# Delta steps: 32-row products of the block inverse joined in pairs, dense sets divided by filter and value products

## The chip, the cores and the metric

The kernel runs on one core of a Trainium2 chip. Its time is device time in microseconds (us), the median of several executions. PE is TensorE (its matmuls), PEld its weight loads, DVE VectorE, ACT ScalarE, POOL GpSimd, and SP the queue that issues the DMAs.

## The reference

Two layers over 16 sequences of 512 tokens of 128 values, each layer an attention part and a feed-forward part. The change lies in the attention of the second layer, a gated delta rule with 16 heads of 64 values:

```python
qkv = silu(causal_conv4(x @ W_qkv));  beta = sigmoid(b);  g = -A * softplus(a + dt_bias)
q = l2norm(q) / 8;  k = l2norm(k)
def step(S, t):                              # per sequence and head, S is 64x64
    S = S * exp(g[t])
    S = S + outer(k[t], (v[t] - k[t] @ S) * beta[t])
    return S, q[t] @ S
y = rmsnorm(y) * norm_w * silu(z);  x = x + y @ W_o
```

## The kernel before

The program has five phases: front (first layer), gates, delta, attention with experts, and capacity. The delta phase walks 64 steps. A step takes one chunk of 64 tokens of two sequences at once (rows 0 to 63 and 64 to 127, `SEQS`), for all 16 heads. Within a chunk the rule becomes the solution of a triangular system of 64 rows per sequence and head, and the kernel builds the inverse of that system from blocks:

- POOL inverts the diagonal blocks of 16 rows (`L1383`, `L1387`), and SP carries blocks between `at`, `ablk`, `tblk`, `ti` and `tt` through DRAM.
- Two blocks of 16 make one of 32. There are two such joins per sequence, `BLOCKS = [(b, u)]`. First `at` times `ti` gives `w4` (L1612, 16 heads by four blocks); DVE masks it with a column of row flags `hi` (L1801). Then `tt` times `w4` (L1634, for `ti`) and `w4` times `tt` (L1638, for `tt`) are made head by head. DVE subtracts the one into `ti` (L1824, `t4_ready`), ACT copies the other negated into `tt` (L1452, `tt4_ready`).
- Two blocks of 32 make the whole: `w5` (L1649, copied by ACT at L1469) and L1659, copied by ACT at L1478. The system is then solved at L1682.

Every fp32 product is two weight loads and two matmuls in PE's stream, so that L1612 has 128 matmuls a step.

In the same step the other engines prepare later steps. The filter of q and k takes four blocks a step (`conv(p, u, e)`, e from 0 to 3, L1542): PE makes the product, ACT takes the last tap out of PSUM (L1406, `take_conv`), DVE adds the other three (L1761, `filter_block`, raising `conv_done`), ACT applies silu (L1418). Blocks 0, 2 and 3 use the same two PSUM banks, block 1 another two, so that `conv` waits at L1540, before block 3 until the filter of block 2 is done:

```python
hold(sem("conv_done"), done - 1 if e == 2 else done)
```

The value products `project_v` (L1567) are two halves of four taps each; `sum_squares` (L1580) is a product of 128 rows and 128 columns that moves two columns.

The order on each engine is written out by hand in `iteration`, and each engine goes through it in order; `hold` and `wait_ge` wait on semaphores. PE's order in a step is: state products (L1561), key products `kkq` (L1552), L1612, filter block 0, values half 0, filter block 1, L1634 with L1638, filter block 2, values half 1, L1649, filter block 3, L1659, z (L1665), `sum_squares(0)`, solve (L1682), transposes, update (L1708), L1561, output (L1717), `sum_squares(1)`, L1734. ACT's order around the filter is: block 0 taken, values half 0, silu of block 0, block 1 taken, the four copies of L1452, block 2 taken, silu of block 1, squares, values half 1, the copy of `w5`, block 3 taken. DVE's order is: L1776 and L1778 twice (which read the key products), L1796, L1801, L1806, L1813, filter of blocks 0 and 1, L1824, filter of block 2, L1832, L1834, L1838, filter of block 3. Steps 1 to 56 run in a loop of eight steps each; the last five steps have no filter products.

Of the kernel before, what the change touches and what calls it, by code (L numbers as in the profile page):

```python
# [6 lines left out]
ALU = mybir.AluOpType  # L7
# [3 lines left out]
P = 128  # L11
# [677 lines left out]
CH = 64  # L689
# [348 lines left out]
def delta_phase(nc, x_in, x_out, h_t, gates, decays, a_blocks, t_blocks, w_in, conv_t, norm_w, w_o):  # L1038
# [17 lines left out]
    with ExitStack() as ctx:  # L1056
# [5 lines left out]
        hi = sb("hi", [P, 1])  # L1062
# [34 lines left out]
        ti = sb("ti", [P, DH, HB + SB])  # L1097
        tt = sb("tt", [P, DH, CH])
        w4 = sb("w4", [P, DH, HB])
# [122 lines left out]
        def _(sp):  # L1222
# [42 lines left out]
            def iteration(p, u):  # L1265
# [33 lines left out]
                if have(p, u + 1):  # L1299
                    hold(sem("inverse"), i + 2)  # L1300
                    sp.dma_start(t_blocks[0].rearrange("n h r c -> (n h) r c"), tblk[:, 0, :, :]).then_inc(sem("ti_stored"), 16)
                    hold(sem("turned_back"), i + 2)
                    sp.dma_start(t_blocks[1].rearrange("n h r c -> (n h) r c"), tblk[:, 1, :, :]).then_inc(sem("tt_stored"), 16)
                    hold(sem("ti_stored"), 16 * (i + 2))
                    hold(sem("w5_sum"), i + 1)
                    for n in range(NBLK):
                        rows = slice(SB * n, SB * n + SB)
                        m = n % (CH // SB)
                        if m != 3:
                            c1 = SB if m == 1 else HB  # L1310
# [19 lines left out]
        def _(pool):  # L1330
# [23 lines left out]
            link(pool.tensor_tensor(hi[:, :], hk[:, 0:1], hk[:, 1:2], ALU.add))  # L1354
# [44 lines left out]
        def _(act):  # L1399
# [31 lines left out]
            def iteration(p, u):  # L1431
# [16 lines left out]
                if now:  # L1448
                    act.wait_ge(sem("t4_sum"), i + 1)
                    for b, w in BLOCKS:  # L1450
                        low = slice(64 * b + HB * w, 64 * b + HB * w + SB)
                        last = act.activation(tt[low, :, HB * w + SB:HB * w + HB],  # L1452
                                              pb[low, 1, DH * SB:2 * DH * SB].rearrange("p (h c) -> p h c", c=SB),
# [56 lines left out]
        def _(pe):  # L1510
# [54 lines left out]
            def project_v(p, u, m):  # L1565
                for t in range(TAPS):
                    last = pe.matmul(pa[:, B + m, :], hs[:, u % 2, t, :], wv[:, t, cols(m)],  # L1567
                                     start=(t == 0), stop=(t == TAPS - 1))
                last.then_inc(sem("v_sum"), 1)
# [14 lines left out]
            def iteration(p, u):  # L1584
# [9 lines left out]
                if then:  # L1594
# [9 lines left out]
                    kkq(p, u + 1, 1)  # L1604
                if now:
# [3 lines left out]
                    for h in range(DH):  # L1609
                        for b, w in BLOCKS:  # L1610
                            rows = rows_of(b, w)
                            last = pe.matmul(pb[rows, 0, h * SB:(h + 1) * SB], at[rows, u % 2, h, HB * w:HB * w + HB],  # L1612
                                             ti[rows, h, HB:HB + SB], start=True, stop=True)
                    last.then_inc(sem("w4_sum"), 1)
                if cv:
                    conv(p, u, 0)
                if then:
# [4 lines left out]
                    project_v(p, u + 1, 0)  # L1622
                if cv:
                    conv(p, u, 1)
                if now:
# [5 lines left out]
                    for h in range(DH):  # L1631
                        for b in SEQS:
                            rows = rows_of(b, 0)
                            last = pe.matmul(pb[rows, 0, (DH + h) * SB:(DH + h + 1) * SB], tt[rows, h, 0:HB], w4[rows, h, 0:SB],  # L1634
                                             start=True, stop=True)
                        for b, w in BLOCKS:
                            rows = rows_of(b, w)
                            last = pe.matmul(pb[rows, 1, (DH + h) * SB:(DH + h + 1) * SB], w4[rows, h, :],  # L1638
                                             tt[rows, h, HB * w + SB:HB * w + HB], start=True, stop=True)
                    last.then_inc(sem("t4_sum"), 1)  # L1640
# [78 lines left out]
                if far:  # L1719
                    hold(sem("n4_ready"), n + 1)  # L1720
                    hold(sem("q_squared"), n + 1)
                    sum_squares(1).then_inc(sem("q_summed"), 1)
                if now:
# [7 lines left out]
                    for m in HALVES:  # L1731
# [5 lines left out]
                        last.then_inc(sem("o_sum"), 1)  # L1737

# [3 lines left out]
        def _(dve):  # L1742
# [40 lines left out]
            def iteration(p, u):  # L1783
# [98 lines left out]
                if far:  # L1882
                    dve.wait_ge(sem("q_summed"), n + 1)
                    dve.tensor_scalar(tq[:, (u + 2) % 4, :], pb[:, 1, DH:2 * DH], DHD * RMS_EPS,
                                      DHD * RMS_EPS * L2_EPS, ALU.mult, ALU.add).then_inc(sem("tq_ready"), 1)
                if now:
# [8 lines left out]
                    last.then_inc(sem("o_ready"), 1)  # L1895
                made[part] += links[0]
# [739 lines left out]
```

## Time and profile before

| | us |
|---|---|
| median of 3 executions | 4637.02 |
| lowest, highest | 4636.9, 4659.84 |
| the profiled execution | 4655.05 |
| its span | 4653.3 |
| delta stage within the span, about | 1410 to 3960 |
| mean granted TensorE clock over the span | 0.897 |

The profile describes the one profiled execution, whose time is 18.03 us above the median. Its parts give the busy time of each engine, groups of instructions by line, waits by what ended them, and timelines. "issue" names idle time for which the profile shows no semaphore. PEclk is the granted TensorE clock: 1.00 is the higher level, 2.4 GHz, and 0.50 the lower, 1.2 GHz; other values are means over a stretch.

### The profile page before, as it was taken

The numbers are of one execution on the slowest core, as the hardware profiler recorded it, in microseconds if no ns is written. First come the engines' busy times: TensorE is split into PE (matmuls) and PEld (weight loads), VectorE is DVE, ScalarE is ACT, GpSimd is POOL, SyncE is SP. The second block draws the span as 40 slices with busy tenths as digits, with TensorE's granted clock in tenths as the row PEclk, the third lists the DMA queues.
The fourth block names the chain that finished last, engine by engine and source line by source line (L and its number), as shares of the span: only waits on it lengthen the run. The fifth ranks groups of instructions, "written<-read, shape, count | busy, mean of one in ns | idle before, by whom it ended". The sixth has DMA issues, their size and how long they took to land. (4 is left out here: it accounts for less than half of the span.)

```text
span 4653.3 us, 163745 instructions
## 1 busy us (share of the span) xinstructions
PE 3861.4 (83%) x66245; PEld 2812.4 (60%) x66245; DVE 3117.4 (67%) x6104; ACT 1733.8 (37%) x3495; POOL 1595.7 (34%) x2519
## 2 busy tenths in 40 slices
PE   6999999866648998989988989989899998588860
PEld 4666666533326776767776767767677766455530
DVE  3777777747746676767666766767677654288858
ACT  1222222224423343444443433434444432277750
POOL 1333333311004454444444444544444443100001
PEclk6998999988858999999999999999999987699975
DMA  0222222136522222222222222222222221111105
GB/s 25 44 47 46 55 56 49 42 84 155 158 65 49 42 56 41 47 51 48 50 47 49 48 49 40 57 42 47 51 48 49 49 47 26 55 27 28 28 18 149
DMA packets 695281, 251.77 MB, mean 54 GB/s; under 512 B 529368, under 2 KB 660128, under 8 KB 694176
## 3 DMA queue, kind: packets, MB, share of 16 engines
q1 hardware_dynamic: 694560, 241.62, 23.7%
q8 instruction: 518, 8.49, 0.8%
q14 instruction: 203, 1.66, 0.1%
HBM read 154.63 MB, written 86.79 MB: 52 GB/s over the span
## 5 line engine op out<-in xcount | busy, mean ns | idle before, releaser
L1373 POOL TENSOR_TENSOR d_f<-d_ms,d_mhalf 128x16 f32<-128x16 f32 x64 | 239.5, 3742 | 965.1 <-DVE d_ms L1807 965.1
L1567 PE MATMUL d_pa<-d_wv,d_hs 128*128 128x512 f32 x1024 | 517.6, 652 | 0.9 <-DVE d_qk L1778 0.4
L1761 DVE SCALAR_TENSOR_TENSOR d_acc<-d_pa,d_cq,d_acc 128x512 f32<-128x512 f32 x576 | 431.7, 750 | 95.2 <-ACT d_acc L1406 80.3
L1383 POOL TENSOR_TENSOR d_prod<-d_ablk,d_tblk 128x15 f32<-128x15 f32 (+7 forms) x960 | 342.5, 357 | 218.5 <-DMA d_ablk<-a_blocks 147.9
L1387 POOL TENSOR_TENSOR d_tblk<-d_tblk,d_prod 128x28 f32<-128x28 f32 (+7 forms) x896 | 336.4, 375 | 70.8 <-POOL d_prod L1383 0.2
L1567 PEld LDWEIGHTS d_pa<-d_wv,d_hs 128*128 128x128 f32 x1024 | 219.5, 215 | 232.1 <-issue 220.2
L1542 PE MATMUL d_pa<-d_hq,d_wqk 128*128 128x259 f32 x768 | 255.4, 462 | 81.4 <-DVE d_acc L1761 58.0
L1406 ACT ACTIVATE d_acc<-d_pa,d_cq 128x512 f32<-128x512 f32 x192 | 131.9, 687 | 420.8 <-PE d_pa L1542 418.0
L262 POOL TENSOR_TENSOR a_act<-a_act,a_cws 128x512 f32<-128x512 f32 x128 | 166.8, 1316 | 310.2 <-DMA a_cws<-cw_rows 165.3
L1580 PEld LDWEIGHTS d_pb<-d_of_head,d_sqT 128*128 128x128 f32 x2048 | 246.2, 196 | 39.2 <-issue 39.0
L1370 POOL TENSOR_TENSOR d_nr<-d_n,d_half_power 128x16 f32<-128x16 f32 x64 | 188.0, 2938 | 193.8 <-DVE d_n L1846 179.8
L1580 PE MATMUL d_pb<-d_of_head,d_sqT 128*128 128x2 f32 x2048 | 243.8, 250 | 0.6 <-ACT d_sqT L1411 0.5
L294 ACT ACTIVATE a_sil<-a_gp 128x512 f32<-128x512 f32 x144 | 86.1, 598 | 406.1 <-PE a_gp L367 403.6
L1761 DVE SCALAR_TENSOR_TENSOR d_acc<-d_pc,d_cq,d_acc 128x512 f32<-128x512 f32 x192 | 144.2, 751 | 130.5 <-ACT d_acc L1406 125.9
L1505 ACT ACTIVATE d_sq<-d_o 128x1024 f32<-128x1024 f32 x64 | 67.7, 1057 | 435.4 <-DVE d_o L1892 390.1
L1542 PEld LDWEIGHTS d_pa<-d_hq,d_wqk 128*128 128x128 f32 x768 | 149.8, 216 | 132.3 <-issue 111.3
L906 PE MATMUL g_pe<-g_gu,g_after 128*128 128x512 f32 x256 | 152.0, 725 | 89.7 <-DVE g_gu L966 89.7
L2208 PE MATMUL e_xp<-e_w,e_yT 128*128 128x512 f32 x256 | 151.6, 676 | 47.8 <-ACT e_part L2094 47.8
L1423 ACT ACTIVATE d_v<-d_pa 128x512 f32<-128x512 f32 x128 | 76.4, 597 | 301.9 <-PE d_pa L1567 288.2
L1418 ACT ACTIVATE d_kq<-d_acc 128x512 f32<-128x512 f32 x256 | 159.5, 623 | 73.1 <-DVE d_acc L1761 72.5
L369 PE MATMUL a_up<-a_bhT,a_wu 128*128 128x512 f32 x288 | 168.7, 671 | 13.3 <-DVE a_act L546 11.8
L1776 DVE TENSOR_TENSOR d_at<-d_dd,d_pa 128x512 f32<-128x512 f32 x128 | 87.6, 684 | 136.6 <-PE d_pa L1552 136.4
(371 smaller groups left out, 9418.3 us busy)
## 6 DMA issues: line engine op xcount, KB each, us to landing
a_cws<-cw_rows SPq DMA_DIRECT2D x32, 1024.0 KB, 10.5
decays<-g_dec SPq DMA_DIRECT2D x16, 2048.0 KB, 7.3
d_dd<-decays SPq DMA_DIRECT2D x64, 512.0 KB, 4.3
d_hs<-h_t SPq DMA_DIRECT2D x512, 32.0 KB, 2.2
t_blocks<-d_tblk SPq DMA_DIRECT2D x128, 128.0 KB, 1.7
a_blocks<-d_at SPq DMA_DIRECT2D x512, 16.0 KB, 1.9
d_ablk<-a_blocks SPq DMA_DIRECT2D x64, 128.0 KB, 2.1
d_tt<-t_blocks SPq DMA_DIRECT2D x512, 16.0 KB
```

Of the source, the lines that this page charges most:

```text
L262: pool.tensor_tensor(act_sb[:, b, :], act_sb[:, b, :], cws[:, m % 2, b, :], ALU.mult)\
L369: pe.matmul(up[:, :], wu[:, b, :], bhT[:, m % 2, :], start=True, stop=True).then_inc(sem("up_sum"), 1)
L906: last = pe.matmul(pe_[:, c % 2, m, :], after[:, :, :].rearrange("p b s -> p (b s)"), gu[:, c % 2, m * DH // 2:(m + 1) * DH // 2, :].rearr ...
L1370: pool.tensor_tensor(nr[:, :], n4[:, :], half_power[:, :], ALU.pow).then_inc(sem("nr_ready"), 1)
L1373: pool.tensor_tensor(f[:, :], ms[:, :], mhalf[:, :], ALU.pow).then_inc(sem("f_ready"), 1)
L1383: link(pool.tensor_tensor(prod[:, 0:n, 0:s + 1], ablk[:, s, s + 1:SB].unsqueeze(2).to_broadcast([P, n, s + 1]), tblk[:, 0, s, 0:s + 1].uns ...
L1387: link(pool.tensor_tensor(tblk[:, 0, s + 1:SB, 0:s + 1], tblk[:, 0, s + 1:SB, 0:s + 1], prod[:, 0:n, 0:s + 1], ALU.subtract))
L1418: act.activation(kq[:, n, j, kind, :, :, :].rearrange("p c b t -> p b c t"), acc[:, e % 2, :].rearrange("p (b c t) -> p b c t", b=2, t=CH) ...
L1542: last = pe.matmul(raw(e)[:, b, 0:QH], wqk[:, col * P:(col + 1) * P], hq[:, n, b, :], start=True, stop=True)
L1567: last = pe.matmul(pa[:, B + m, :], hs[:, u % 2, t, :], wv[:, t, cols(m)], start=(t == 0), stop=(t == TAPS - 1))
L1580: last = pe.matmul(pb[:, 1, DH * kind + 2 * j:DH * kind + 2 * j + 2], sqT[:, kind, j, :], of_head[:, :], start=True, stop=True)
L1761: last = dve.scalar_tensor_tensor(out=own, in0=raw(e)[:, :, t:t + QT], scalar=cq[:, t, col:col + 1], in1=own, op0=ALU.mult, op1=ALU.add)
```

## The change

- The two joins of a sequence become one product. `fourths` (for L1612) takes 64 rows and 64 columns of `at` and moves 32 columns of `ti`: 64 matmuls a step in place of 128. `joined` (for L1638) takes 64 by 64 of `w4` and moves 32 columns of `tt`: 64 in place of 128. `joined_back` is L1634 as it was, 64 matmuls.
- For this, `ti` and `w4` are 64 columns wide, two SP loads of `ti` go to other columns, and DVE masks `w4` with both columns of `hk` over 128x512 (before: `hi` over 128x256). ACT reads the joined result with another stride.
- `fourths` moves behind filter block 0.
- Values half 1 is divided by taps: `joined(0)`, tap 0, `joined(1)`, tap 1, `joined_back`, taps 2 and 3. Filter block 2, which stood ahead of this half, now follows it.
- `sum_squares(1)` moves behind L1734 on PE, and its reader `tq` behind `o_ready` on DVE.

```diff
+            def fourths(u, m):
+                for h in range(HH * m, HH * m + HH):
+                    for b in SEQS:
+                        last = pe.matmul(pb[rows_of(b), 0, h * HB:(h + 1) * HB], at[rows_of(b), u % 2, h, :],
+                                         ti[rows_of(b), h, HB:CH], start=True, stop=True)
+            def joined(m):
+                for h in range(HH * m, HH * m + HH):
+                    for b in SEQS:
+                        last = pe.matmul(pb[rows_of(b), 1, h * HB:(h + 1) * HB], w4[rows_of(b), h, :],
+                                         tt[rows_of(b), h, :].rearrange("p (w c) -> p w c", w=2)[:, :, SB:HB],
+                                         start=True, stop=True)
...
+                if cv:
+                    conv(p, u, 0)
                 if now:
                     hold(sem("ti_loaded"), 16 * 6 * (i + 1))
                     if past:
                         hold(sem("x_used"), i - 1 + X_AHEAD)
-                    for h in range(DH):
-                        for b, w in BLOCKS:
...
+                    fourths(u, 0)
+                    fourths(u, 1).then_inc(sem("w4_sum"), 1)
-                if cv:
-                    conv(p, u, 0)
...
+                    joined(0)
+                if then:
+                    project_v(u + 1, 1, (0,))
+                if now:
+                    joined(1)
+                if then:
+                    project_v(u + 1, 1, (1,))
+                if now:
+                    joined_back(0)
+                    joined_back(1).then_inc(sem("t4_sum"), 1)
+                if then:
+                    project_v(u + 1, 1, (2, 3))
                 if cv:
                     conv(p, u, 2)
-                if then:
-                    project_v(p, u + 1, 1)
                 if now:
                     hold(sem("t4_ready"), i + 1)
...
-                    dve.tensor_scalar(w4[:, :, 0:SB], pb[:, 0, 0:DH * SB].rearrange("p (h c) -> p h c", c=SB), hi[:, 0:1],
-                                      None, ALU.mult).then_inc(sem("w4_ready"), 1)
+                    dve.tensor_tensor(w4[:, :, :].rearrange("p h (w c) -> p h w c", w=2)[:, :, :, 0:SB],
+                                      pb[:, 0, :].rearrange("p (h w c) -> p h w c", w=2, c=SB),
+                                      hk[:, :].unsqueeze(1).unsqueeze(3).to_broadcast([P, DH, 2, SB]), ALU.mult)\
+                       .then_inc(sem("w4_ready"), 1)
```

## Rows read from the trace of the kernel before

**Rows 1.** The page: busy us of engines and instructions; the queue that carries instructions.
```profile
PE 3861.4 (83%) x66245; PEld 2812.4 (60%) x66245; DVE 3117.4 (67%) x6104; ACT 1733.8 (37%) x3495; POOL 1595.7 (34%) x2519
...
q8 instruction: 518, 8.49, 0.8%
```

**Rows 2.** Windows of four consecutive delta steps and of the whole delta stage.
```profile
core 0: us, PE busy (x) PEld busy (x) DVE busy (x) ACT busy (x) POOL busy (x), PEclk, DMA share, GB/s
1535.40:1571.70 36.30, 35.13 (x932) 27.92 (x933) 28.22 (x40) 16.06 (x26) 19.48 (x34) 1.00 0.21 46
1571.70:1616.90 45.20, 39.33 (x933) 30.14 (x933) 28.55 (x40) 15.95 (x26) 18.88 (x34) 0.89 0.24 45
...
1652.00:1692.10 40.10, 37.02 (x934) 28.54 (x934) 28.63 (x40) 15.94 (x26) 19.07 (x34) 0.96 0.28 55
1410.00:3960.00 2550.00, 2317.73 (x57764) 1809.08 (x57756) 1699.85 (x2418) 993.60 (x1552) 1186.99 (x2144) 0.94 0.24 47
```

**Rows 3.** Waits of PE in the delta stage: total us, times, longest.
```profile
PE d_pb L1612 <- issue: 64.4, 45, 2.6
PE d_pb L1638 <- issue: 38.4, 17, 3.0
```

**Rows 4.** Waits of PE from 1571.7 to 1692.1 us (three steps).
```profile
PE d_pb L1612 <- issue: 3.9, 2, 2.2
PE d_pb L1638 <- issue: 2.7, 1, 2.7
```

**Rows 5.** Timeline of PE within one set: start us, us, line, count.
```profile
2534.02 1.01 PE L1612 MATMUL d_pb<-d_ti,d_at 32*32 32x16 f32 x87
2537.16 0.53 PE L1612 MATMUL d_pb<-d_ti,d_at 32*32 32x16 f32 x41 [2.14 <-issue]
```

**Rows 6.** Timeline of PE in an even step (from 2576.4 us).
```profile
2576.35 1.98 PE L1552 MATMUL d_pa<-d_kq 64*64 64x128 f32 x64
2578.26 1.40 PE L1612 MATMUL d_pb<-d_ti,d_at 32*32 32x16 f32 x128
2579.93 1.11 PE L1542 MATMUL d_pa<-d_hq,d_wqk 128*128 128x259 f32 x4 [0.27 <-issue]
...
2587.42 1.13 PE L1542 MATMUL d_pa<-d_hq,d_wqk 128*128 128x259 f32 x4
...
2591.92 1.20 PE L1649 MATMUL d_pb<-d_ti,d_at 32*32 32x32 f32 x64
2593.07 1.11 PE L1542 MATMUL d_pa<-d_hq,d_wqk 128*128 128x259 f32 x4
2594.65 1.20 PE L1659 MATMUL d_pb<-d_tt,d_w 32*32 32x32 f32 x64 [0.46 <-ACT d_w L1469]
```

**Rows 7.** Groups of PE in that step: busy us, mean ns.
```profile
L1580 PE MATMUL d_pb<-d_of_head,d_sqT 128*128 128x2 f32 x32 | 3.7, 246 | 0.0
...
L1638 PE MATMUL d_pb<-d_tt,d_w 32*32 32x16 f32 x128 | 2.2, 183 | 0.0
...
L1682 PE MATMUL d_pc<-d_r,d_tt 64*64 64x64 f32 x64 | 2.1, 220 | 0.0
```

**Rows 8.** Timeline of DVE in that step.
```profile
2578.12 0.68 DVE L1778 TENSOR_TENSOR d_qk<-d_dd,d_pa 128x512 f32<-128x512 f32 x1
...
2590.60 2.32 DVE L1761 SCALAR_TENSOR_TENSOR d_acc<-d_pa,d_cq,d_acc 128x512 f32<-128x512 f32 x3
```

**Rows 9.** Timeline of ACT in that step.
```profile
2581.16 0.69 ACT L1406 ACTIVATE d_acc<-d_pa,d_cq 128x512 f32<-128x512 f32 x1 [4.01 <-PE d_pa L1542]
```

**Rows 10.** Timeline of PE in a late step without filter products.
```profile
3819.74 1.20 PE L1649 MATMUL d_pb<-d_ti,d_at 32*32 32x32 f32 x64
3822.48 1.69 PE L1659 MATMUL d_pb<-d_tt,d_w 32*32 32x32 f32 x64 [1.54 <-ACT d_w L1469]
```

**Rows 11.** Windows behind such a wait, two late steps.
```profile
3782.00:3792.50 10.50, 8.96 (x194) 6.88 (x188) 2.78 (x7) 4.21 (x7) 8.65 (x22) 0.84 0.11 33
3820.50:3831.00 10.50, 8.96 (x112) 6.75 (x106) 1.36 (x1) 3.38 (x5) 6.77 (x20) 0.61 0.10 30
```

More of the change, by code:

```diff
@@ L1061, in delta_phase @@
         hk = sb("hk", [P, 2])
-        hi = sb("hi", [P, 1])
         of_head = sb("of_head", [P, 2])
@@ L1096, in delta_phase @@
         prod = sb("prod", [P, SB, SB])
-        ti = sb("ti", [P, DH, HB + SB])
+        ti = sb("ti", [P, DH, CH])
         tt = sb("tt", [P, DH, CH])
-        w4 = sb("w4", [P, DH, HB])
+        w4 = sb("w4", [P, DH, CH])
         w5 = sb("w5", [P, DH, HB])
@@ L1309, in iteration @@
                         if m != 3:
-                            c1 = SB if m == 1 else HB
+                            c1 = (HB, SB, HB + SB)[m]
                             sp.dma_start(ti[rows, :, c1:c1 + SB], t_blocks[0, n, :, :, :].rearrange("h r c -> r h c"))\
@@ L1452, in iteration @@
                         last = act.activation(tt[low, :, HB * w + SB:HB * w + HB],
-                                              pb[low, 1, DH * SB:2 * DH * SB].rearrange("p (h c) -> p h c", c=SB),
+                                              pb[low, 1, :].rearrange("p (h w c) -> p h w c", w=2, c=SB)[:, :, w, :],
                                               ACT.Copy, scale=-1.0)
@@ L1563, in against_state, with project_v, joined_back @@
                 return last
-            def project_v(p, u, m):
-                for t in range(TAPS):
+            def project_v(u, m, taps):
+                for t in taps:
                     last = pe.matmul(pa[:, B + m, :], hs[:, u % 2, t, :], wv[:, t, cols(m)],
                                      start=(t == 0), stop=(t == TAPS - 1))
-                last.then_inc(sem("v_sum"), 1)
+                if TAPS - 1 in taps:
+                    last.then_inc(sem("v_sum"), 1)
+            def fourths(u, m):
[3 more added lines that the diff above has]
+                                         ti[rows_of(b), h, HB:CH], start=True, stop=True)
+                return last
+            def joined(m):
[4 more added lines that the diff above has]
+                                         start=True, stop=True)
+                return last
+            def joined_back(m):
+                for h in range(HH * m, HH * m + HH):
+                    for b in SEQS:
+                        rows = rows_of(b, 0)
+                        last = pe.matmul(pb[rows, 0, (DH + h) * SB:(DH + h + 1) * SB], tt[rows, h, 0:HB], w4[rows, h, 0:SB],
+                                         start=True, stop=True)
+                return last
             def turn_keys(u):
@@ L1608, in iteration @@
                         hold(sem("x_used"), i - 1 + X_AHEAD)
-                    for h in range(DH):
-                        for b, w in BLOCKS:
[L1611 to L1614, printed above, removed]
-                if cv:
-                    conv(p, u, 0)
+                    fourths(u, 0)
+                    fourths(u, 1).then_inc(sem("w4_sum"), 1)
                 if then:
@@ L1621, in iteration @@
                     hold(sem("qk_read"), 2 * k + 2)
-                    project_v(p, u + 1, 0)
+                    project_v(u + 1, 0, range(TAPS))
                 if cv:
@@ L1630, in iteration @@
                         hold(sem("n4_ready"), k + 1)
[L1631 to L1640, printed above, removed]
+                    joined(0)
[10 more added lines that the diff above has]
+                    project_v(u + 1, 1, (2, 3))
                 if cv:
                     conv(p, u, 2)
-                if then:
-                    project_v(p, u + 1, 1)
                 if now:
@@ L1718, in iteration @@
                     last.then_inc(sem("out_ready"), 1)
[L1719 to L1722, printed above, removed]
                 if now:
@@ L1737, in iteration @@
                         last.then_inc(sem("o_sum"), 1)
+                if far:
+                    hold(sem("n4_ready"), n + 1)
+                    hold(sem("q_squared"), n + 1)
+                    sum_squares(1).then_inc(sem("q_summed"), 1)
             steps(pe, iteration)
@@ L1881, in iteration @@
                     dve.tensor_tensor(xo[:, :], xt[:, :], pb[:, 0, 0:D], ALU.add).then_inc(sem("x_used"), 1)
[L1882 to L1885, printed above, removed]
                 if now:
@@ L1895, in iteration @@
                     last.then_inc(sem("o_ready"), 1)
+                if far:
+                    dve.wait_ge(sem("q_summed"), n + 1)
+                    dve.tensor_scalar(tq[:, (u + 2) % 4, :], pb[:, 1, DH:2 * DH], DHD * RMS_EPS,
+                                      DHD * RMS_EPS * L2_EPS, ALU.mult, ALU.add).then_inc(sem("tq_ready"), 1)
                 made[part] += links[0]
```

1 line of the change is left out of this document (removed).

## The prediction

> **What bounds the kernel now.** The page first [rows 1]: PE is busy 3861.4 of 4653.3 us, DVE 3117.4. That says PE, but an average hides the stages, so the next view is the windows [rows 2]. The reader is to see there that the delta stage takes 2550 us for 64 steps, 39.8 us each, and that its steps are of two sorts. The one from 1535.4 takes 36.3 us at a granted clock of 1.00, with PE busy 35.13. The one from 1571.7 takes 45.2 us at 0.89 with the same work (932 and 933 matmuls). So an unhindered step is PE's own work, and a slow one is PE standing still and then clocked down.
>
> The waits of PE tell what it stood for [rows 3]: 64.4 us ahead of L1612 and 38.4 ahead of L1638, released by "issue", no semaphore. Both are sets of small matmuls. The timeline shows one such wait inside a set [rows 5]: 87 matmuls of L1612, 2.14 us of nothing, then the other 41. Nothing in the source waits there. The instruction queue moved 8.49 MB in 518 packets, for 132,490 matmuls and weight loads [rows 1]: 64 bytes each, 256 to a packet. I read the wait as PE having run through its instructions faster than packets come. L1612 is 256 instructions in 1.40 us [rows 6], 183 a us; the stage's mean is 115,520 in 2550 us [rows 2], 45 a us.
>
> What a wait costs beyond itself: the steps of 45.2 and 40.1 us are 12.7 us longer than two of 36.3 [rows 2], and hold 3.9 + 2.7 = 6.6 us of these waits [rows 4]. The rest, 6.1 us, is the lower clock behind them (0.89 and 0.96). So the 102.8 us of the stage [rows 3] stand for 102.8 x 12.7 / 6.6 = 198 us.
>
> A rule speaks against this reading. The Trainium skill, Runtime: NRT & Kernel Launch, Instruction fetch mechanics, gives TensorE an instruction memory of 128 KiB, 2048 instructions, refilled in blocks of 256, with the fetch mostly hidden. By it a set of 256 could not starve, and the 198 us would stay. The packet size agrees; the wait after 87 matmuls of a set does not. It is the last of the cases below.
>
> **What goes.** 64 products fewer a step are 256 PE instructions, and the dense stretches are broken up: filter block 0 stands ahead of `fourths`, a long product (one tap of the values, four instructions) between the halves of `joined` and one ahead of `joined_back`, `sum_squares(1)` ahead of the state products. Where 384 instructions of small matmuls ran in 2.2 us (L1638 with L1634 [rows 7], twice 192), no more than 128 now follow each other. I take the whole 198 us as gained. The waits at L1561 where the loop starts again, and in update with state products, are as before.
>
> **What the pairs cost.** Fewer is not shorter. A product whose weights have 128 columns and which moves two columns takes 3.7 / 32 = 0.115 us [rows 7], so here the load sets the pace, about 0.9 ns a column. `fourths` loads 64 columns to move 32, on two tiles. L1682 loads 64 and moves 64 on the same two tiles: 64 matmuls in 2.08 us (2.1 in [rows 7]); half of 0.115 us on two tiles at once would be 1.84 us. I take 1.95 us against 1.40 for L1612 [rows 6]: +0.55. `joined` has the same form, 1.95 us, and `joined_back`, two tiles with 32 columns, I take as L1649, 1.20 us [rows 6]. That is 3.15 against 2.2 for L1634 and L1638 together [rows 7]: +0.95. Bounds: from below, all at the pace of L1612, 1.40 us / 128 = 11 ns a matmul, 2.1 us in all, which is 1.5 less than before; from above, the pace of L1682, 5.4 us, 1.8 more. DVE's wider mask is hidden: DVE would wait there anyway.
>
> **What the order costs.** *Filter block 0.* It waits for the first read of the key products on DVE, which ends at 2578.80 [rows 8]; these products end at 2578.33 [rows 6]. L1612 filled that time. PE waits 0.55 us with the hand-over, and the 0.27 us of issue behind L1612 go [rows 6]: +0.28. Behind the waiting block stand `fourths` and all of PE; the `ti` loads only gain time.
>
> *Filter block 3.* This is the large one. It waits until ACT has taken block 2 and DVE has filtered it. Before, values half 1 and L1649 lay between the two, and block 3 began at 2593.07, just when DVE's filter ended, at 2592.92 [rows 6, 8]. Now only L1649 lies between them. From the end of block 2: ACT 0.69 us [rows 9], DVE 2.32 us [rows 8], and three hand-overs, 0.12 (PE at 2581.04 to ACT at 2581.16 [rows 6, 9]), some 0.03 from ACT to DVE, 0.15 back to PE [rows 6, 8]: 3.31 us. L1649 covers 1.13 of it. PE stands still for 2.18 us in every step that has filter products. Nothing shortens this: DVE and ACT are waiting for block 2 too. Behind block 3 stand L1659, z, the sums and the solve, so the whole step is that much later.
>
> *L1659* no longer waits for the copy of `w5`, which ends about when block 3 does: -0.46 us [rows 6]. *`sum_squares(1)` and `tq`* change places with work of the same length; the key products' second half gets its PSUM banks sooner, and `tq` is needed only in the next step: nothing.
>
> Sum for a step: 0.55 + 0.95 + 0.28 + 2.18 - 0.46 = 3.5 us. Steps with filter products are those up to 58, so 59 (`have_conv`): 206.5 us. The five others have the pairs alone, 1.5 - 0.27: 6 us.
>
> **The clock behind the new wait.** In late steps PE already waits 1.54 us at this place, between L1649 and L1659 [rows 10]. In the 10.5 us that follow, the granted clock is 0.84 in one and 0.61 in another [rows 11]: 1.7 and 4.1 us of work lost. Behind the issue waits it was 45.2 x 0.11 / 2 = 2.5 us each with two waits in a step, 1.6 with one [rows 2]. So a still PE next to L1649's small matmuls brings the lower level (1.2 GHz). I take 2.5 us, and a fall in 50 of the 59 steps, since the longer wait may sometimes be harmless: 125 us. Bounds: nothing, and 59 x 4.1 = 242 us.
>
> **The sum.** -198 + 206.5 + 6 + 125 = +140 us on the profiled execution, 4655.05, which makes 4795. The median of the runs is 18.03 lower: **4777 us**.
>
> **The rivals.** *The wait stays, the clock holds.* For it: the steps of 36.3 us keep 1.00 through waits of 0.46 us, and 64x64 sets give PE more to do than 32x32 ones. Against it: 1.54 us was enough [rows 10, 11]. Without the 125 us: 4652 us, no change.
>
> *The pairs are cheap.* Faster than before: if the loads of a set overlap so well that only issue counts, 11 ns a matmul, each step is 3.0 us shorter than I say, 64 times, 193 us: 4584 us. It decides from about 15 ns a matmul (5.1 us of sets less 140 / 64 = 2.2, over 192 matmuls). For it: L1612 itself, 11 ns on four tiles. Against it: on two tiles L1649 takes 19 ns and L1682, with the same loads, 32.
>
> *The starvation is not one.* If the waits at L1612 and L1638 come from something else than the supply, they stay: 4777 + 198 = 4975 us. For it: no row names their cause. Against it: they fall inside sets, at the densest places. (The Trainium skill's rule on instruction fetch, above, would have it so.)
>
> **How the numbers follow.** The likeliest, wait and lower clock: 0.60, between 4700 and 4900. Wait without the clock: 0.13. Cheap pairs: 0.20. No gain: 0.07. The range reaches down to the cheap pairs with the clock falling, 4575, and up to the pace of L1682 (16 us more) with a fall in every step (117 more), 4910; below it lie cheap pairs at a full clock, above it the fourth case. 0.5% is 23 us, about what a measurement of this kernel can tell from no change. Slower by more: 0.67 (the first case and the last); within it: 0.12 (nearly all of the second); faster: 0.21 (the third and a little of the second).
>
> **What would show it.** Right: no issue waits at the two sets; a wait of about 2.2 us before filter block 3 in PE's waits, 59 times, released by DVE's filter, some 125 us in all; sets of 1.9 to 2.1 us; steps of about 40 us at 1.00 and 42 below it, all alike where they used to alternate. Wrong: block 3 starting right behind L1649, sets near 1 us, or steps at 1.00 throughout.

## The result and the profile after

The changed kernel takes 4874.65 us (median of four runs, 4870.05 to 4883.51) against 4636.96 for the kernel before: 1.0507 times as long, 95% interval 1.0466 to 1.0548. The forecast was 4777 with a range of 4575 to 4910: the direction and the range held, and the time is 98 us above the likeliest value. The profiled execution has a span of 4872.5 us (before 4653.3) at a mean granted clock of 0.888 (before 0.897).

The page after: PE's busy time, and the instruction queue with packets and MB [rows 1].
```profile
PE 4084.3 (84%) x58053; PEld 2968.5 (61%) x58053; DVE 3116.0 (64%) x6104; ACT 1730.2 (36%) x3495; POOL 1590.0 (33%) x2518
...
q8 instruction: 453, 7.42, 0.7%
```
PE issues 8192 matmuls fewer, which is 128 matmul records in each of the 64 steps (a product counts twice, as 64 products of L1612 stand as x128 in [rows 6]), and is busy for 223 us more. Fewer instructions are not less time here.

The waits of PE after, from 1400 to 4200 us (total us, times, longest), beside [rows 3]. L1540 is a filter block, L1782 DVE's filter, L1799 DVE's read of the key products.
```profile
PE d_pa L1540 <- DVE d_acc L1782: 123.8, 59, 2.1
PE d_pa L1540 <- DVE d_qk L1799: 31.9, 52, 0.6
PE d_pc L1559 <- issue: 28.7, 12, 3.6
...
PE d_pb L1680 <- ACT d_w L1467: 8.3, 5, 1.8
```
The two issue waits ahead of the sets, 102.8 us, are gone. In their place stand a wait of 2.1 us ahead of filter block 3 in every one of the 59 steps with filter products, and one of 0.6 us ahead of filter block 0 in most of them.

The timeline of PE in one step, from filter block 0 to block 3 [rows 6]. L1574 is `fourths`, L1565 a values tap, L1582 half of `joined`, L1592 `joined_back`, L1670 the second-level set (L1649 before).
```profile
2113.59 1.11 PE L1540 MATMUL d_pa<-d_hq,d_wqk 128*128 128x259 f32 x4 [0.63 <-DVE d_qk L1799]
2114.63 2.05 PE L1574 MATMUL d_pb<-d_ti,d_at 64*64 64x32 f32 x64
...
2121.12 1.12 PE L1582 MATMUL d_pb<-d_tt,d_w 64*64 64x32 f32 x32
2122.17 1.12 PE L1565 MATMUL d_pa<-d_wv,d_hs 128*128 128x512 f32 x2
...
2125.34 1.19 PE L1592 MATMUL d_pb<-d_w,d_tt 32*32 32x16 f32 x64
2126.45 1.98 PE L1565 MATMUL d_pa<-d_wv,d_hs 128*128 128x512 f32 x4
2128.28 1.04 PE L1540 MATMUL d_pa<-d_hq,d_wqk 128*128 128x259 f32 x4
2129.24 1.20 PE L1670 MATMUL d_pb<-d_ti,d_at 32*32 32x32 f32 x64
2132.54 1.11 PE L1540 MATMUL d_pa<-d_hq,d_wqk 128*128 128x259 f32 x4 [2.10 <-DVE d_acc L1782]
```
The reader is to see the chain of the forecast in the last three rows: block 2 ends at 2129.3, only L1670 is left to run, and block 3 waits for DVE's filter of block 2.

Windows after: one step, a stretch of it that begins 1.1 us behind the start of its filter block 3 (2311.11), and the 59 steps with filter products; then the same 59 steps before (columns as in [rows 2]; the third number from the end, ahead of the DMA share, is the granted clock).
```profile
2289.60:2336.70 47.10, 44.10 (x808) 34.74 (x809) 28.35 (x40) 15.95 (x25) 18.82 (x34) 0.86 0.20 39
2312.20:2325.90 13.70, 13.70 (x156) 11.44 (x156) 6.56 (x11) 5.12 (x8) 6.23 (x7) 0.50 0.15 29
...
1406.60:4005.80 2599.20, 2389.56 (x45953) 1844.40 (x45953) 1615.76 (x2305) 939.08 (x1474) 1100.78 (x2006) 0.92 0.22 43
```
```profile
1409.10:3764.30 2355.20, 2149.95 (x53501) 1679.65 (x53502) 1616.54 (x2305) 942.50 (x1474) 1113.60 (x2011) 0.95 0.24 48
```
The stretch runs at the lower of the two levels, 1.2 GHz (0.50); it is one of the longest. In the 59 steps after there are 61 stretches at this level, 7.2 us long in the mean; in the same steps before there are 46, 5.3 us long. I call such a stretch a fall of the clock. From a row of the 59 steps three parts follow: idle PE (length less PE's busy time), the loss at the lower level (length times one less the clock, good to 12 us), and the rest, PE's work at the full clock. I use them for the kernels below. They describe the profiled execution, which lies up to 28 us off the median of its kernel.

| 59 steps, us | length | idle | lost to the clock | work |
|---|---|---|---|---|
| before | 2355 | 205 | 118 | 2032 |
| after | 2599 | 210 | 208 | 2182 |
| difference | +244 | +5 | +90 | +150 |

### The profile page after: what moved, and what is told of

It is laid out like the page before. It is cut to its first block and busy times, and to the rows that moved or that the text cites. A ratio compares the mean times of both kernels' runs of the same rounds, so it can differ in the third digit from the quotient of the medians.

```text
span 4872.5 us, 147360 instructions
## 1 busy us (share of the span) xinstructions
PE 4084.3 (84%) x58053; PEld 2968.5 (61%) x58053; DVE 3116.0 (64%) x6104; ACT 1730.2 (36%) x3495; POOL 1590.0 (33%) x2518
## 5 line engine op out<-in xcount | busy, mean ns | idle before, releaser
L1782 DVE SCALAR_TENSOR_TENSOR d_acc<-d_pa,d_cq,d_acc 128x512 f32<-128x512 f32 x576 | 431.5, 749 | 197.6 <-ACT d_acc L1404 183.7
L1565 PE MATMUL d_pa<-d_wv,d_hs 128*128 128x512 f32 x1024 | 507.1, 618 | 0.4 <-DVE d_qk L1799 0.4
L1540 PE MATMUL d_pa<-d_hq,d_wqk 128*128 128x259 f32 x768 | 235.9, 434 | 220.1 <-DVE d_acc L1782 183.5
L1385 POOL TENSOR_TENSOR d_tblk<-d_tblk,d_prod 128x28 f32<-128x28 f32 (+7 forms) x896 | 371.3, 414 | 70.1
L1381 POOL TENSOR_TENSOR d_prod<-d_ablk,d_tblk 128x15 f32<-128x15 f32 (+7 forms) x960 | 317.6, 331 | 108.3 <-DMA d_ablk<-a_blocks 24.1
L1540 PEld LDWEIGHTS d_pa<-d_hq,d_wqk 128*128 128x128 f32 x768 | 146.8, 205 | 288.5 <-issue 274.2
L1605 PEld LDWEIGHTS d_pb<-d_of_head,d_sqT 128*128 128x128 f32 x2048 | 272.4, 210 | 59.6 <-issue 55.2
L1605 PE MATMUL d_pb<-d_of_head,d_sqT 128*128 128x2 f32 x2048 | 265.5, 260 | 0.1
L1565 PEld LDWEIGHTS d_pa<-d_wv,d_hs 128*128 128x128 f32 x1024 | 173.6, 189 | 133.8 <-issue 124.3
L1686 PE MATMUL d_pa<-d_wz,d_hs 128*128 128x512 f32 x256 | 218.4, 1004 | 0.0
L1782 DVE SCALAR_TENSOR_TENSOR d_acc<-d_pc,d_cq,d_acc 128x512 f32<-128x512 f32 x192 | 144.2, 751 | 89.0 <-ACT d_acc L1404 84.5
```

The lines of the kernel that those rows point to most:

```text
L1381: link(pool.tensor_tensor(prod[:, 0:n, 0:s + 1], ablk[:, s, s + 1:SB].unsqueeze(2).to_broadcast([P, n, s + 1]), tblk[:, 0, s, 0:s + 1].uns ...
L1385: link(pool.tensor_tensor(tblk[:, 0, s + 1:SB, 0:s + 1], tblk[:, 0, s + 1:SB, 0:s + 1], prod[:, 0:n, 0:s + 1], ALU.subtract))
L1540: last = pe.matmul(raw(e)[:, b, 0:QH], wqk[:, col * P:(col + 1) * P], hq[:, n, b, :], start=True, stop=True)
L1605: last = pe.matmul(pb[:, 1, DH * kind + 2 * j:DH * kind + 2 * j + 2], sqT[:, kind, j, :], of_head[:, :], start=True, stop=True)
L1686: last = pe.matmul(pa[:, B + m, :], hs[:, (u + 1) % 2, TAPS - 1, :], wz[:, cols(m)], start=True, stop=True)
L1782: last = dve.scalar_tensor_tensor(out=own, in0=raw(e)[:, :, t:t + QT], scalar=cq[:, t, col:col + 1], in1=own, op0=ALU.mult, op1=ALU.add)
```

## The experiments

The first four runs take the change apart: is it the place of filter block 2, the pairs, or the order?

**E1, filter block 2 ahead of taps 2 and 3** (from the changed kernel).
```
+                if cv:
+                    conv(p, u, 2)
                 if then:
                     project_v(u + 1, 1, (2, 3))
-                if cv:
-                    conv(p, u, 2)
```


> The changed kernel with filter block 2's product directly behind the joined sets, ahead of values taps 2 and 3 of half 1 (1.98 us). Theory A (the loss is the wait ahead of filter block 3, 123.8 us, and the clock that falls behind it): VectorE starts the filter of block 2 about 2 us earlier, the wait ahead of block 3 falls below 15 us in all, the mean granted clock rises above 0.90, and the time is 4600 to 4680 us. Rival B (the clock falls because of the paired sets themselves, which hold few columns for their time): the wait goes but the clock stays at 0.89 and the time is about 4875 - 124 = 4750 us.

Measured: 4652.76 us, ratio to before 1.0028 (1.0009 to 1.0047). Window of the 59 steps:
```profile
1405.50:3777.30 2371.80, 2236.14 (x45950) 1744.75 (x45950) 1619.21 (x2305) 935.54 (x1474) 1097.06 (x2009) 0.98 0.24 47
```
Its waits:
```profile
PE d_pa L1540 <- DVE d_acc L1782: 51.8, 59, 0.9
```
222 us come back from moving four matmuls past four others. The 59 steps are 227 us shorter: 74 us less idle, 161 us less lost to the clock (208 to 47), the work the same within the error. Theory A; only its "below 15 us" was too hopeful, for 0.9 us is left of each wait. Behind none of these 59 waits of 0.9 us does the clock fall (within 3 us of its end), and it stays at 0.98 in the mean.

**E2, filter block 2 late in the kernel before**: the same move alone, in the other direction.
```
-                if cv:
-                    conv(p, u, 2)
                 if then:
                     project_v(p, u + 1, 1)
+                if cv:
+                    conv(p, u, 2)
```


> The kernel before with one edit: filter block 2's product behind values half 1 instead of ahead of it; all 32-row products stay. Theory A: a wait of about 2 us ahead of filter block 3 appears 59 times (about 120 us), the clock falls behind it in most steps (about 125 us more), and the time is about 4637 + 245 = 4880 us, as slow as the changed kernel. Rival B (a wait alone costs its own length, the clock's fall comes from the paired sets): 4637 + 120 = 4760 us.

Measured: 4912.34 us, ratio 1.0613 (1.0566 to 1.0661). Waits, and the window of the 59 steps:
```profile
PE d_pa L1542 <- DVE d_acc L1761: 127.0, 60, 3.2
PE d_pb L1612 <- issue: 61.6, 41, 2.6
...
PE d_pb L1638 <- issue: 33.6, 17, 2.4
```
```profile
1409.70:4005.20 2595.50, 2304.86 (x53501) 1771.93 (x53501) 1607.52 (x2305) 934.22 (x1474) 1046.98 (x2006) 0.89 0.22 44
```
A move of four matmuls costs 276 us with no pair in the kernel. Idle grows by 85 us (127 for the new wait, less 27 of the wait of L1659 that it covers and 8 at the two sets; the other 7 were not followed up), the loss to the clock by 168 (118 to 286). So the clock takes twice what the added idle itself takes.

**E3, the pairs alone**: the paired products in the old order. On PE only the sets themselves differ from the kernel before (the wider `ti`, `w4`, mask and reads come along, and all of `joined` now stands ahead of `joined_back`, where the two went head by head):
```
                 if now:
                     hold(sem("ti_loaded"), 16 * 6 * (i + 1))
                     ...
+                    fourths(u, 0)
+                    fourths(u, 1).then_inc(sem("w4_sum"), 1)
                 if cv:
                     conv(p, u, 0)
                 ...
+                    joined(0)
+                    joined(1)
+                    joined_back(0)
+                    joined_back(1).then_inc(sem("t4_sum"), 1)
                 if cv:
                     conv(p, u, 2)
                 if then:
                     project_v(u + 1, 1, range(TAPS))
```


> The paired products of the changed kernel in the order of the kernel before: fourths ahead of filter block 0, joined sets undivided, filter block 2 ahead of the four values taps, sums of squares where they were. Theory A: no issue waits at the sets (102.8 us before), no wait ahead of filter block 3; sets longer by 0.65 + 1.2 us a step, 59 steps, 109 us: about 4637 - 198 + 109 = 4550 us, from 4520 to 4600. Rival B (the paired sets bring the clock down by themselves): 4700 us or more. Rival C (starvation comes back when the sets are not divided): issue waits of over 40 us at the sets and about 4650 us.

Measured: 4541.94 us, ratio 0.98 (0.9766 to 0.9835): 95 us faster than before. Timeline of a step (L1664 is the second-level set, L1674 the set behind filter block 3), two groups of PE from 1410 to 3660 us (busy, mean ns, idle before), and the window of the 59 steps:
```profile
1610.33 2.06 PE L1582 MATMUL d_pb<-d_tt,d_w 64*64 64x32 f32 x64
1612.32 1.19 PE L1592 MATMUL d_pb<-d_w,d_tt 32*32 32x16 f32 x64
1613.43 1.15 PE L1540 MATMUL d_pa<-d_hq,d_wqk 128*128 128x259 f32 x4
1614.42 3.59 PE L1565 MATMUL d_pa<-d_wv,d_hs 128*128 128x512 f32 x8
1617.94 1.20 PE L1664 MATMUL d_pb<-d_ti,d_at 32*32 32x32 f32 x64
...
1620.67 1.20 PE L1674 MATMUL d_pb<-d_tt,d_w 32*32 32x32 f32 x64 [0.46 <-ACT d_w L1467]
```
```profile
L1574 PE MATMUL d_pb<-d_ti,d_at 64*64 64x32 f32 x3776 | 124.7, 220 | 4.4 <-DMA d_ti<-t_blocks 4.3 <-issue 0.2
...
L1582 PE MATMUL d_pb<-d_tt,d_w 64*64 64x32 f32 x3776 | 121.2, 220 | 0.0
```
```profile
1409.20:3659.80 2250.60, 2156.21 (x45949) 1738.27 (x45950) 1632.31 (x2305) 944.38 (x1474) 1105.24 (x2011) 0.99 0.26 50
```
Theory A; rivals B and C fall: 64 joined matmuls in one piece, with the 64 of `joined_back` behind them, do not starve, and the clock is 0.99. The work rises by 102 us (2032 to 2134), 1.73 a step: the pairs do take longer, and what they save is idle (205 to 94) and clock (118 to 23).

**E4, the order alone**: the changed kernel's order with the 32-row products. From the changed kernel (`joined` in the same way):
```
                 for h in range(HH * m, HH * m + HH):
-                    for b in SEQS:
-                        last = pe.matmul(pb[rows_of(b), 0, h * HB:(h + 1) * HB], at[rows_of(b), u % 2, h, :],
-                                         ti[rows_of(b), h, HB:CH], start=True, stop=True)
+                    for b, w in BLOCKS:
+                        rows = rows_of(b, w)
+                        last = pe.matmul(pb[rows, 0, h * SB:(h + 1) * SB], at[rows, u % 2, h, HB * w:HB * w + HB],
+                                         ti[rows, h, HB:HB + SB], start=True, stop=True)
```


> The order of the changed kernel with the 32-row products of the kernel before (fourths behind filter block 0, sets divided by values taps, filter block 2 behind all of them, sums of squares last). Theory A: the wait ahead of filter block 3 is there as in the changed kernel (about 2 us, 59 times) with its clock falls, and because the number of instructions is that of before, 50 to 100 us of issue waits stay at the sets: about 4637 + 245 + 20 = 4900 us. Rival D (dividing the sets is enough to end the starvation): issue waits under 20 us, about 4780 us; then the pairs themselves cost time.

Measured: 4828.01 us, ratio 1.04 (1.0362 to 1.0438), 47 us below the changed kernel. Groups of PE from 1410 to 3660 us (busy, mean ns, idle before): `joined` with 32 rows, then `fourths`.
```profile
L1586 PE MATMUL d_pb<-d_tt,d_w 32*32 32x16 f32 x6656 | 75.6, 180 | 0.0
L1577 PE MATMUL d_pb<-d_ti,d_at 32*32 32x16 f32 x6656 | 65.5, 180 | 0.0
```
No issue waits at these two sets, and 4.9 us in all at `joined_back`, with all the instructions of before: rival D in that, theory A in the wait (126.9 us ahead of block 3). Spacing alone ends the starvation, at least in steps as slow as these. The time is between the two expectations.

The next runs ask whether idle is what brings the clock down, and what the rest of the order costs.

**E6, work put into the wait**: the changed kernel computes L1670 twice, the same values to the same place.
```
-                    for h in range(DH):
+                    for h in 2 * list(range(DH)):
                         for b in SEQS:
                             last = pe.matmul(pb[rows_of(b, 1), 0, h * HB:(h + 1) * HB], ...
```


> The changed kernel with the second-level set ahead of filter block 3 computed twice, the same values into the same place: 64 more TensorE instructions pairs' worth of 1.2 us in each of the 64 steps, 77 us of added work. Theory A (the clock falls behind the idle wait of 2.1 us): the added work lies in the wait, which shrinks to about 0.9 us with its end where it was, the clock then falls in few steps, and the kernel becomes faster although it does more: 4875 - 100 to 150 = 4725 to 4775 us. Rival B (the falls have nothing to do with the wait's idle): clock stays at 0.89 and the time at 4865 to 4890 us. Rival C (the added work isn't hidden): 4950 us.

Measured: 4769.52 us, ratio to before 1.0287 (1.0239 to 1.0336): 105 us faster than the changed kernel, with more work in it. Timeline and window:
```profile
1471.03 2.21 PE L1670 MATMUL d_pb<-d_ti,d_at 32*32 32x32 f32 x128
1474.33 1.11 PE L1540 MATMUL d_pa<-d_hq,d_wqk 128*128 128x259 f32 x4 [1.08 <-DVE d_acc L1782]
```
```profile
1413.30:3868.80 2455.50, 2329.04 (x49725) 1821.88 (x49726) 1619.67 (x2305) 935.76 (x1474) 1090.37 (x2006) 0.97 0.23 46
```
Block 3 starts no earlier (3.30 us behind the start of L1670, as in the changed kernel), yet the steps are 144 us shorter: 83 us less idle and 134 less lost to the clock, for 73 more of work. Theory A: PE's standing still is what brings the lower level here; of the 61 falls 28 are left, and the clock falls behind 16 of the 59 waits that are left, most of them of 1.1 us, against 53 of the 59 of 2.1 us in the changed kernel. It is not the only thing that does: of the 22 falls in E5, below, 20 have no wait of over 0.25 us in the 2.6 us ahead of them. (In the profiled executions 35 us of the gain are lost again outside these steps: some 5 to the doubled set in the last five, 28 to the clock, which costs 357 us there against 329, and between 316 and 359 in the other runs.)

**E5, the joined sets undivided**, filter block 2 behind them, the other moves kept. In the changed kernel `joined(0)`, `joined(1)`, `joined_back`, `conv(p, u, 2)` and `project_v(u + 1, 1, range(TAPS))` follow each other.

> The changed kernel with its joined sets undivided and filter block 2 directly behind them, ahead of all four values taps of half 1; the fourths stay behind filter block 0 and the sums of squares stay last. Theory A (dividing by taps costs 0.65 us a step, and the wait of 0.9 us ahead of filter block 3 that is left with filter block 2 ahead of two taps goes with four taps): 4653 - 38 - 52 = 4563 us, from 4540 to 4590, with the wait of filter block 0 for VectorE's weighing (about 30 us in all) as what still separates it from the paired products in the old order (4542). Rival B (the new places of the fourths and of the sums of squares cost by themselves): over 4600 us.

Measured: 4606.07 us, ratio 0.9933 (0.9915 to 0.9951): the time of rival B, outside the range of theory A. Waits of PE from 1400 to 4200 us (L1674 is the set behind block 3, L1793 the read called L1799 above):
```profile
PE d_pb L1674 <- ACT d_w L1467: 35.0, 64, 1.5
...
PE d_pa L1540 <- DVE d_qk L1793: 28.9, 48, 0.6
```
The division with its rest of a wait costs 47 us (E1 less E5) where I had expected 90; 27 of the difference is the wait of the set behind block 3 for ScalarE's copy, which is 8.3 us in the changed kernel and in E1, and 35.0 here, since no wait of block 3 covers it any more. And E5 lies 64 us above E3, with only the wait of filter block 0 (28.9 us) to show for it; E11 parts this.

**E11, sums of squares last** with the pairs in the old order, the fourths ahead of filter block 0: in E3, `sum_squares(1)` goes behind the last products of a step, and its reader on DVE behind `o_ready`.

> The paired products in the old order (4542 us) with the sums of squares of the queries put last as in the changed kernel; with the fourths moved too it was 4606 us. Theory A (the fourths' new place is what costs: filter block 0 is then the instruction that waits for VectorE's weighing, 29 us, with clock falls behind it): 4535 to 4555 us here. Rival F (the place of the sums of squares costs, by the clock at the turn of the step): 4580 us or more.

Measured: 4558.22 us, ratio 0.9813 (0.9781 to 0.9846). So the sums' place costs 16 us, which the overlapping intervals of E3 and E11 do not tell from nothing, and the fourths' place 48, of which the wait of filter block 0 is some 30; the rest is open. Nearer to theory A, 3 us above its range.

**E7, the order with filter block 2 ahead, 32-row products**: E4 with the edit of E1.

> The order of the changed kernel with the 32-row products of before, and with filter block 2 ahead of values taps 2 and 3, so that the long wait ahead of filter block 3 is gone. Theory D (spacing of the sets by long instructions is what ends the starvation; the pairs aren't needed for it and cost 0.65 + 1.2 us a step): no issue waits at the sets, and 4653 - 109 = 4545 us, from 4520 to 4590. Rival E (in the slow order the fetch kept up only because a step took 44 us; at 38 us it needs the smaller number of instructions): issue waits of 40 us or more at the sets, their clock falls, and 4620 us or more.

Measured: 4587.71 us, ratio 0.99 (0.9861 to 0.994). One row of its groups from 1410 to 3660 us, `joined_back`; the two other sets have an idle of 0.0 in front of them:
```profile
L1595 PE MATMUL d_pb<-d_w,d_tt 32*32 32x16 f32 x3712 | 70.6, 178 | 4.5 <-issue 4.4
```
In steps of 39 us the spacing still does it: theory D, at the upper edge of its range. Against E1, whose one difference is the pairs, it is 65 us faster, where I had taken 109 for the pairs. Once the order spaces the sets, the pairs only cost.

**E9, the 32-row products with the two moves alone** (fourths behind block 0, sums last; E4 with the joined sets undivided as in E5, so that all of `joined` stands ahead of `joined_back` as in E3).

> The 32-row products of before, joined sets undivided with filter block 2 directly behind them and all four values taps behind it; only two moves of the changed kernel are left: the fourths behind filter block 0 and the sums of squares last. Theory D (the two moves alone put enough long instructions between the dense sets that the fetch keeps up, with all 256 instructions more): no issue waits over 10 us at either set; the same order with pairs took 4606 us, less 1.85 us x 59 = 109: 4497 us, from 4480 to 4540. Rival E (the joined sets need the division or the pairs): the 17 issue waits of 38 us ahead of the joined set stay and bring the clock down, 4560 to 4620 us.

Measured: 4593.74 us, ratio 0.9913 (0.9885 to 0.9941). Its largest sum of issue waits at a set:
```profile
PE d_pb L1595 <- issue: 40.4, 22, 3.4
```
Rival E: undivided and unpaired, the joined sets starve, now in `joined_back`; `fourths`, behind filter block 0, does not. With E3 and E7: pairs or division, either is enough at the joined sets, and the change did both.

**E10, the keys' product against the state between the halves of the key products**, on E9 (the three added lines stood at the head of the step):
```
                     kkq(p, u + 1, 0)
+                if now and carried(u):
+                    hold(sem("state_ready"), carries(p, u))
+                    against_state(u, keys, pc).then_inc(sem("ks"), 1)
```


> The same kernel with the keys' product against the state (1.2 us) moved between the two halves of the products of keys and queries, so that VectorE has 1.2 us more to weigh the first half before filter block 0 wants its place: the wait of 0.6 us in front of filter block 0 (28 us in all) goes. Theory: 28 to 45 us faster than the kernel without this move (with it the clock falls near that wait go too). Rival: the denser run of small products in front of the fourths costs as much in issue waits, no difference within 10 us.

Measured: 4564.71 us, ratio 0.9837 (0.9802 to 0.9872), 29 us less than E9, the lower edge of what was expected. The wait of filter block 0 is gone from the first rows of the waits; issue waits of 16.9 us have come up at `fourths`, which now follows the same instructions without the 0.6 us pause:
```profile
PE d_pb L1595 <- issue: 44.8, 29, 3.5
...
PE d_pb L1577 <- issue: 16.9, 23, 2.3
```

**E12, filter block 2 between `joined` and `joined_back`**, on E10.
```
                     joined(1)
+                if cv:
+                    conv(p, u, 2)
+                if now:
                     joined_back(0)
                     joined_back(1).then_inc(sem("t4_sum"), 1)
-                if cv:
-                    conv(p, u, 2)
```


> The kernel with the 32-row products, the two moves and the keys' product between the halves (4565 us), and filter block 2's four long instructions put between the joined products and the products back, where 44.8 us of issue waits lay. Theory D (long instructions between dense sets are what the fetch needs, wherever they come from): the issue waits at the products back fall below 15 us and the time is 4490 to 4535 us, below the paired products in the old order (4542). Rival E (the stall is set by the number of instructions in the stretch and moves to the next set): issue waits of 40 us or more elsewhere at the sets and 4550 to 4580 us.

Measured: 4547.56 us, ratio 0.9805 (0.9769 to 0.984).
```profile
PE d_pb L1595 <- issue: 22.3, 17, 2.1
...
PE d_pb L1577 <- issue: 15.4, 24, 1.8
```
Half of the issue waits at `joined_back` stay, and nearly all of those at `fourths`: four long instructions (1.1 us) space the sets, but not by enough. It meets neither expectation, and ends where E3 is, within the intervals.

**E8, half of the gate product ahead of the set that waits for ScalarE**, on E3 (z is the gate product):
```
+                if then:
+                    hold(sem("v_taken"), 2 * k + 2)
+                    pe.matmul(pa[:, B, :], hs[:, (u + 1) % 2, TAPS - 1, :], wz[:, cols(0)], start=True, stop=True)
                 if now:
                     hold(sem("w5_ready"), i + 1)
```


> The paired products in the old order (4542 us) with the first half of the gate product (0.65 us at the full clock) put ahead of the set that waits for ScalarE's copy of the second-level sums (34.8 us of waits in 64 places, 0.43 us in a full step). Theory A: the half lies in that wait, 59 x 0.43 = 25 us go: 4515 us, from 4500 to 4530. Rival B (the set then ends 0.2 us later, and what waits for its copy, the solve, moves as much as is gained): 4535 to 4550 us.

Measured: 4668.15 us, ratio 1.006 (1.0032 to 1.0088): 126 us slower than E3, which neither expectation had. Its wait, the timeline of a step, then the window of a stretch in it and of the 59 steps. L1677 is the set, L1681 the second half of z, L1605 the sums of squares.
```profile
PE d_pb L1605 <- ACT d_tt L1476: 40.8, 62, 0.8
```
```profile
1582.58 1.20 PE L1677 MATMUL d_pb<-d_tt,d_w 32*32 32x32 f32 x64
1583.71 1.12 PE L1681 MATMUL d_pa<-d_wz,d_hs 128*128 128x512 f32 x2
1585.46 2.35 PE L1605 MATMUL d_pb<-d_of_head,d_sqT 128*128 128x2 f32 x16 [0.63 <-ACT d_tt L1476]
```
```profile
1586.80:1593.60 6.80, 6.80 (x81) 6.67 (x81) 2.07 (x6) 1.71 (x3) 4.15 (x5) 0.50 0.28 56
...
1398.20:3795.00 2396.80, 2292.51 (x45953) 1856.61 (x45953) 1619.73 (x2305) 944.15 (x1474) 1092.02 (x2011) 0.93 0.24 47
```
The wait moved rather than went: 0.46 us ahead of the set became 0.63 ahead of the sums. That alone is a few us; idle in the steps is 104 against 94. But the clock fell from 0.99 to 0.93, 145 us (the profiled executions differ by 139). The work is the same, in another order. Within 3 us of the new wait, which stands between the second half of z and the sums of squares, the clock falls in 53 of 60 cases; behind the wait of 0.46 us in E3 (ahead of the set, with the whole of z behind it) in none of 59. Whether the wait or the halved product ahead of it does this was not parted.

## Why the forecast held, and where it was off

The whole change is the sum of five steps, taken in this order, each the difference of two runs above; in another order the same edit costs otherwise (the pairs save 95 us here and cost 65 between E7 and E1):

| edit | us | from |
|---|---|---|
| pairs in the old order | -95 | before 4637 to E3 4542 |
| sums of squares last (intervals overlap) | +16 | to E11 4558 |
| fourths behind filter block 0 | +48 | to E5 4606 |
| joined sets divided by taps | +47 | to E1 4653 |
| filter block 2 behind taps 2 and 3 | +222 | to the changed kernel 4875 |

- **The issue waits go, with their clock**: right, also in size. E3 has 111 us less idle and 95 less lost to the clock than the kernel before, 206 against the 198 of the forecast. Both fewer instructions (E3) and long ones between the sets (E4, E7) end the waits of [rows 3]; what the forecast could not tell is that either is enough. That the supply is the cause can be read from the trace of before: each of the 46 issue waits of over 0.7 us at these sets in the 59 steps ends 1.2 to 1.6 us after a packet of the instruction queue has ended, while 9% of all moments lie that far behind one; and in the 14 steps that have two such waits the second comes 511 to 513 instructions of PE behind the first, which is two packets. So the third rival (the starvation is not one) falls. The rule of the Trainium skill (Runtime: NRT & Kernel Launch, Instruction fetch mechanics) by which a set of 256 instructions would not starve is not borne out by these waits.
- **The pairs cost time**: right, with the sets 2.05 us for `fourths` (1.95 said), 2.06 for `joined` in one piece (E3; 1.95 said) and 1.19 for `joined_back` (1.20 said). From the start of one row to the start of the next (the rows of a timeline overlap by up to 0.2 us) that is 1.99 and 3.10 us, against 1.40 and 2.14 in the kernel before: 1.55 us a step, 1.5 said. The rival of cheap pairs falls; E7 beside E1 gives 65 us as what the pairs cost where nothing starves.
- **Filter block 3 waits for DVE's filter of block 2**: right in place, number and length, 59 times 2.10 us against 2.18, and E1 and E2 show that this one place decides.
- **The wait of filter block 0**: right in kind, 0.63 us (0.55 said).
- **The taps**: not in the sum. I costed the division at nothing, since the same instructions run. From the start of `joined` to the start of the second-level set they take 7.61 us in one piece each (E3, 1610.33 to 1617.94) and 8.12 divided (2121.12 to 2129.24): 0.51 us a step, 30 us. The work rose by 61 us more than the 1.5 us a step of the forecast (150 against 88.5). Of the other 31, 3 are the pairs' 0.05 us a step; values half 0 and the sums of squares, which now stand behind a set of small matmuls, take 0.1 us longer each (3.70 against 3.59 in E3, 1.95 against 1.84), 12 us; the last 16 are open, and two readings of the work, each good to 12 us, can hide them.
- **The clock**: the mis-sized term. By the forecast 95 of the old 118 us would go and 125 come, 148 us; there are 208. The number of falls was right: of the 59 waits of 2.1 us 53 bring one, between the start of the wait and 3 us behind its end, and I took 50. Their length was not: 7.1 us in the mean (13.7 the longest), 3.5 us lost each, where I took 2.5 from the shorter waits of before. In E2, with no pair in the kernel, 54 of the 59 waits bring one of 6.9 us, so the pairs are not what makes them long; what does was not tried. The rival in which the clock holds falls.

Idle came out near the forecast (+5 against -102.8 + 59 x 2.0 = +15). So in the 59 steps +244 stand against +134: 60 us more of clock, 61 more of work, 10 less of idle. The range held without large errors that cancel. (By the medians it is 98 and not 110, since these differ by 238 and the forecast had 6 us outside these steps.)

One sign of the forecast did not come: the steps are not alike. Read from the second-level set of one step to that of the next, 3 of 57 run at 1.00, in 39.5 to 41.1 us (40 said); the others take 41.1 to 49.6 us, by how long the clock stays down, and all of them 44.0 in the mean.

Of the versions that are faster than both kernels the two fastest are the pairs in the old order (E3, 4542 us) and the 32-row products with four moves (E12, 4548 us). E12 still has 38 us of issue waits at the sets; a better spacing there was not tried.

## What to carry to other kernels

Ahead of an edit to an in-order engine, follow each consumer: four matmuls that lost their cover cost 276 us (E2), more than the 95 that the pairs save in the old order (E3). Price a wait on PE with the clock that falls behind it, which here took another 1.6 to 2.2 times the idle that came or went (E6, E2, E1), and it depends on the place as well as on the length (E8). If PE starves for instructions, one remedy was enough here: fewer of them, or enough long ones between them (E7; the four of E12 were too few); paying for both bought nothing (E1 beside E7).

## What the runs showed of the hardware

The price of a set is not in its shape. In E3 two sets have 64 matmuls of 64x64 each:
```profile
1625.39 2.08 PE L1697 MATMUL d_pc<-d_r,d_tt 64*64 64x64 f32 x64
...
1628.43 1.16 PE L1723 MATMUL d_pc<-d_y,d_ktok 64*64 64x64 f32 x64
```
By the source the first alternates between two tiles (rows and columns of the same sequence), the second goes through four (rows of a sequence, columns of a head). The pairs brought `fourths` from four tiles of 32 to two of 64: 1.40 us for 128 matmuls before, 2.05 for 64 after. That the tiles are the cause is read from the source and not tried.

Work added in front of a wait can make a kernel faster (E6, 105 us), and a wait of 0.63 us can cost more than one of 0.9 (E8 beside E1), by where it stands. Ahead of filter block 3 the clock fell behind none of 59 waits of 0.9 us (E1), 16 of 59 that mostly took 1.1 us (E6), and 53 of 59 of 2.1 us (the changed kernel).
